# First layer: row sums of the softmax weights on GpSimd for four of eight heads, and the output projections spread over those heads

## The chip, the core and the metric

The kernel runs on one core of a Trainium2 chip. TensorE multiplies matrices, VectorE, ScalarE and GpSimd work on elements, and SyncE issues the DMAs. The metric is the device time of one execution in microseconds.

## What is computed

Two layers on x of 8 x 512 x 1024 (batch, channel, token), in float32. The first is group norm, attention with 8 heads of 64 channels, a projection and a residual; the second picks 256 tokens of each batch and runs attention over them. The change touches the first alone:

```python
h = _group_norm(x, gn_w, gn_b)
hf = h.reshape(B, C, N)
qkv = jnp.einsum('oc,bcn->bon', qkv_w, hf) + qkv_b[None, :, None]
...
attn = jnp.einsum('bhdi,bhdj->bhij', q, k) * HEAD_DIM ** (-0.5)
attn = jax.nn.softmax(attn, axis=-1)
out = jnp.einsum('bhij,bhdj->bhdi', attn, v)
...
out = jnp.einsum('oc,bcn->bon', proj_w, out) + proj_b[None, :, None]
return x + out.reshape(B, C, H, W)
```

## The kernel before

To keep float32 accuracy every operand is split into a high part that TensorE takes as it is and a low part, the rest. A product is high x high, high x low and low x high.

The first layer is one long pipeline of 512 steps: 8 batches x 8 heads x 8 steps, t = 8 h + s. In this text "head 3" is the fourth of its batch (h % 8 == 3), and T is the moment at which TensorE begins a step. A step handles 256 keys of 512 queries, so four steps are a half of a head. Per step TensorE (`step`, L477) does, in this order:

- `weigh_low(t-2)` (L473): two matmuls, p_low with the values, into the one bank `pv`;
- `scores(t)` (L446, L450): four matmuls into a ring of two; `take_max(..., 0)` (L427): one matmul of scores, the other way round, of a tile three steps ahead, for the row maxima;
- the units that the plan `PARTS` puts there: a half of a q, k, v or output ("o") projection, 12 matmuls (L371 to L373), in one step or spread over two; "vt", four transposes of v (L382); "g", group sums (L394);
- `weigh_high(t-1)` (L466, L467): four matmuls, p_high with v_high and v_low; `take_max(..., 1)` (L427).

So a step has 12 matmuls of 512 columns, and 18 or 24 with a unit. Units and row-max tiles share three banks of PSUM (2 KB in each partition). `assign_banks` gives them out by position in the matmul order, and `fill_free` makes TensorE wait until the former holder has been read.

v_high has the weights [v, 1] for each head, so that rows 0 to 63 of `pv` come out as the numerators and 64 to 127 as the denominators, every one the same sum of p (for odd heads the other way round); v_low has zeros for the ones.

ScalarE (`step`, L621): every fourth step it copies `pv` to num_den (`numer_denom`, L562); then `exps`: exp of the scores to p_high (L543) and again to p_full (L546), and the high parts of units (L575, L584, L589). VectorE (`step`, L799), one step behind: row_max of the former step's second tile (L679), every fourth step `top_of_halves` (row_max_top, L687), `p_low` = p_full - p_high (L695), row_max of this step's first tile, then the low parts of the units of the step before (q and k L708, two instructions; v L717; the residual of "o" L737), group statistics (`tile_stats`, L780), `o_low` (L792) and in step 3 `reciprocal` (L797). Each engine runs its list in order, so that what is late delays all behind it.

After a head SyncE brings the denominators into columns (`den_to_columns`), VectorE inverts them, SyncE spreads them through DRAM over the 64 rows (`rec_to_row`, `rec_to_rows`), and GpSimd multiplies (`normalise`, L878). That is nearly all that GpSimd does in this layer. Its result goes to `o_high`, `o_low` and the "o" units of the next batch, which lie in head 1 (seven whole ones) and step 0 of head 2. The reading of p_full by `p_low` is what lets ScalarE write it again two steps later.

## Time and profile before

| | us |
|---|---|
| median of 3 runs | 2790.56 (2786.41 to 2794.03) |
| the profiled execution | 2791.04 |
| its span in the profile | 2789.2 |
| TensorE (PE) busy | 2639.5, 95% |
| VectorE (DVE) busy | 2103.8, 75% |
| ScalarE (ACT) busy | 1571.9, 56% |
| GpSimd (POOL) busy | 239.1, 9% |

The first layer's steps run from 47.8 to about 2230 us of the span. Matmuls overlap in the pipeline: one is shown as some 390 ns, but the next starts about 0.23 us after it, so prices of matmuls are read from starts. Where an engine waits in the middle of an instruction (for a port, not for a semaphore), the profile shows no idle time but a longer instruction.

### The profile page before, as it was taken

The numbers are of one execution on the slowest core, as the hardware profiler recorded it, in microseconds if no ns is written. First come the engines' busy times: TensorE is split into PE (matmuls) and PEld (weight loads), VectorE is DVE, ScalarE is ACT, GpSimd is POOL, SyncE is SP. The second block draws the span as 40 slices with busy tenths as digits, with TensorE's granted clock in tenths as the row PEclk, the third lists the DMA queues.
The fourth block names the chain that finished last, engine by engine and source line by source line (L and its number), as shares of the span: only waits on it lengthen the run. The fifth ranks groups of instructions, "written<-read, shape, count | busy, mean of one in ns | idle before, by whom it ended". The sixth has DMA issues, their size and how long they took to land.

```text
span 2789.2 us, 33182 instructions
## 1 busy us (share of the span) xinstructions
PE 2639.5 (95%) x11856; PEld 2192.5 (79%) x11856; DVE 2103.8 (75%) x3294; ACT 1571.9 (56%) x1930; POOL 239.1 (9%) x134
## 2 busy tenths in 40 slices
PE   6999999999999999999999999999999985989998
PEld 5788887888888888888888888888888764777776
DVE  6888768876887688778877887688768856788753
ACT  3767646764676467656765676467656732333321
POOL 1001001100100010000000000000000121000100
PEclk9999999999999999999999999999999997999999
DMA  4522241213122412231223132312122162655443
GB/s 159 170 58 76 57 125 47 80 54 125 47 79 58 125 46 81 61 118 46 84 58 118 46 88 54 118 51 83 54 87 88 53 238 103 227 198 181 172 153 143
DMA packets 154849, 279.48 MB, mean 100 GB/s; under 512 B 51776, under 2 KB 52032, under 8 KB 154176
## 3 DMA queue, kind: packets, MB, share of 16 engines
q1 hardware_dynamic: 152128, 268.98, 30.6%
q0 software_dynamic: 2560, 8.39, 0.9%
q8 instruction: 96, 1.57, 0.2%
q14 instruction: 65, 0.53, 0.1%
HBM read 180.04 MB, written 63.18 MB: 87 GB/s over the span
## 4 chain that ended last, share of the span: by engine, by line
PE 76%; DVE 15%; issue 4%; DMA 2%; ACT 1%; SPq 1%; POOL 0%; DVEq 0%; POOLq 0%; ACTq 0%
PE tiles L371 8%; PE tiles L372 8%; PE tiles L427 8%; PE tiles L373 8%; PE tiles L473 7%; PE tiles L450 7%; PE tiles L466 7%; PE tiles L467 7%; PE tiles L446 7%; DVE p_low L695 4%; PE tiles L1304 4%; DVE row_max L679 2%; PE tiles L1354 2%; DVE flags L1546 1%; DVE flags L1544 1%
## 5 line engine op out<-in xcount | busy, mean ns | idle before, releaser
L679 DVE TENSOR_REDUCE row_max<-tiles 128x1 f32<-128x512 f32 x1014 | 695.7, 687 | 412.5 <-PE tiles L427 407.9
L543 ACT ACTIVATE p_high<-tiles 128x1024 fp32r<-128x1024 f32 x512 | 525.8, 1027 | 616.2 <-PE tiles L450 615.5
L695 DVE TENSOR_TENSOR p_low<-p_full,p_high 128x1024 fp32r<-128x1024 f32 x512 | 667.8, 1304 | 6.0 <-ACT p_full L546 5.2
L546 ACT ACTIVATE p_full<-tiles 128x1024 f32<-128x1024 f32 x512 | 521.7, 1019 | 0.0
L427 PE MATMUL tiles<-k_high_low,q_high_high 128*128 128x512 f32 x1014 | 409.7, 404 | 7.5 <-DVE row_max L679 6.9
L466 PE MATMUL tiles<-p_high,v_high 128*128 128x512 f32 x1024 | 406.8, 397 | 2.1 <-ACT num_den L562 1.3
L467 PE MATMUL tiles<-p_high,v_low 128*128 128x512 f32 x1024 | 402.2, 393 | 0.0
L427 PEld LDWEIGHTS tiles<-k_high_low,q_high_high 128*128 128x128 f32 x1014 | 313.0, 309 | 63.6 <-DVE row_max L679 22.0
L473 PE MATMUL tiles<-p_low,v_high 128*128 128x512 f32 x1024 | 326.5, 400 | 15.5 <-DVE p_low L695 15.3
L878 POOL TENSOR_TENSOR o_normed<-num_den,o_normed 64x1024 f32<-64x1024 f32 x64 | 164.4, 2569 | 2050.1 <-DMA o_normed<-rec_rows 2050.1
L450 PE MATMUL tiles<-q_low_max,k_high_one 65*128 65x512 f32 x1024 | 325.6, 399 | 0.9 <-DMA q_low_max<-row_max_top 0.8
L371 PE MATMUL tiles<-h_high,w_high 128*128 128x512 f32 x768 | 305.0, 397 | 17.6 <-DVE row_max L679 8.6
L446 PE MATMUL tiles<-q_high_high,k_high_low 128*128 128x512 f32 x1024 | 317.2, 391 | 0.0
L372 PE MATMUL tiles<-h_low,w_high 128*128 128x512 f32 x768 | 302.2, 394 | 0.0
L373 PE MATMUL tiles<-h_high,w_low 128*128 128x512 f32 x768 | 301.1, 392 | 0.0
L446 PEld LDWEIGHTS tiles<-q_high_high,k_high_low 128*128 128x128 f32 x1024 | 192.4, 188 | 47.1
L450 PEld LDWEIGHTS tiles<-q_low_max,k_high_one 65*128 65x128 f32 x1024 | 193.5, 189 | 44.1 <-DMA q_low_max<-row_max_top 2.6
L473 PEld LDWEIGHTS tiles<-p_low,v_high 128*128 128x128 f32 x1024 | 190.0, 189 | 46.7 <-DVE p_low L695 27.1
L466 PEld LDWEIGHTS tiles<-p_high,v_high 128*128 128x128 f32 x1024 | 192.8, 188 | 38.4 <-ACT num_den L562 2.2
L467 PEld LDWEIGHTS tiles<-p_high,v_low 128*128 128x128 f32 x1024 | 192.5, 188 | 37.9
L371 PEld LDWEIGHTS tiles<-h_high,w_high 128*128 128x128 f32 x768 | 146.2, 190 | 43.9 <-issue 24.2
L373 PEld LDWEIGHTS tiles<-h_high,w_low 128*128 128x128 f32 x768 | 145.5, 189 | 32.3
(167 smaller groups left out, 3169.9 us busy)
## 6 DMA issues: line engine op xcount, KB each, us to landing
x_tiles<-in_x SPq DMA_DIRECT2D x64, 512.0 KB, 4.8
w_high<-w_split SPq DMA_DIRECT2D x126, 256.0 KB, 2.8
w_low<-w_split SPq DMA_DIRECT2D x126, 256.0 KB, 2.9
k_high_one<-k_high_low SPq DMA_DIRECT2D x128, 128.0 KB, 2.3
q_high_high<-q_high_high SPq DMA_DIRECT2D x128, 128.0 KB, 2.3
o_normed<-rec_rows SPq DMA_DIRECT2D x64, 256.0 KB, 3.7
x<-x_tiles SPq DMA_DIRECT2D x32, 512.0 KB, 4.0
...
```

Of the source, the lines that this page charges most:

```text
L371: mm(fill[:, :], w1, high[:, c, cols], start=(c == 0), stop=False)
L372: mm(fill[:, :], w1, low[:, c, cols], start=False, stop=False)
L373: last = mm(fill[:, :], w2, high[:, c, cols], start=False, stop=(c == CT - 1))
L427: mm(max_bank(h, i, n)[:, :], q1[:, q_slot(h), first:first + HALF - 3:4], k1[:, k_slot(h), n * HALF:(n + 1) * HALF], start=True, stop=True ...
L446: mm(out[:, n * HALF:(n + 1) * HALF], k1[:, wk, keys[n]], q1[:, wq, queries], start=True, stop=False)
L450: last = mm(out[:, n * HALF:(n + 1) * HALF], k2[0:HD + 1, wk, keys[n]], q2[0:HD + 1, wq, queries], start=False, stop=True)
L466: mm(pv[:, :], weights_of(v1, t, n), p, start=(t % 4 == 0 and n == 0), stop=False)
L467: last = mm(pv[:, :], weights_of(v2, t, n), p, start=False, stop=False)
L473: last = mm(pv[:, :], weights_of(v1, t, n), pl[:, t % 2, n * HALF:(n + 1) * HALF], start=False, stop=(t % 4 == 3 and n == 1))
L543: nc.scalar.activation(ph[:, r, :], ring[:, r, :], ACT.Exp, scale=ATT_SCALE).then_inc(s_ph, 1)
L679: nc.vector.reduce_max(mcol[:, h % 2, n, i:i + 1], max_bank(h, i, n)[:, :], AX_X).then_inc(s_mx, 1)
L695: tt(pl[:, r, :], p32[:, r, :], ph[:, r, :].bitcast(F32), ALU.subtract).then_inc(s_pl, 1)
```

## The change

In heads 0 to 3 of each batch the denominators no longer come from ones among the weights:

- TensorE: `v_parts` holds [low, high, one] per head. With [low, high] as weights one matmul of p_high gives both products in the two halves of `pv`, so `weigh_high` has two matmuls for four. In heads 4 to 7 its two become [high, one] and, for 64 rows only, [low].
- ScalarE copies one half of `pv` to `numerators`, VectorE adds the other (`numerators`, in steps 1 and 5, before `p_low`).
- GpSimd adds the p_full tiles of a half: three adds of 128x1024 (`add_up`) and one of 128x512 (`add_tiles`), each after the `p_low` of its step. ScalarE's exp to p_full waits for the add that reads the old content.
- A unit "d" (four transposes, in step 6 and in step 2 of the next head) turns the sums, and VectorE's `denominators` sums them over 128 columns into den_columns. In heads 4 to 7 the denominators are copied alone, as one row, and come by two DMAs.
- The "o" units lie in steps 9 to 23 after the batch's start, most of them spread over two steps; k, q and v of pair 1 and a tile_stats come later; `o_high`, `o_low` of pair 0, `store` of the last tile, `reciprocal`, `rec_to_row`, `rec_to_rows` move by some steps. `normalise` waits for the `p_low` of step 4.

The planner's lists (`READ_BEHIND`, the counts in `bank_events`) and the waits of the second layer's first units are adapted to it. The diff, cut:

```diff
+SUMMED = (0, 1, 2, 3)
...
 PAIR_STEPS = (begins(0, 1, 6, 8, 2, 3, 3, 5, whole=(("k", 0), ("k", 1), ("v", 0), ("q", 1))),
-              begins(1, 3, 5, 8, 10, 12, 12, 14),
+              begins(3, 4, 9, 10, 12, 13, 14, 15, whole=(("k", 0), ("q", 0), ("v", 0))),
               begins(0, 3, 6, 8, 10, 12, 12, 14),
               begins(2, 4, 6, 8, 10, 12, 12, 14))
+OUTPUT_STEPS = {(0, 0): (9, True), (0, 1): (10, False), (1, 0): (12, False), (1, 1): (14, False), (2, 0): (16, True),
+                (2, 1): (17, False), (3, 0): (22, True), (3, 1): (23, False)}
...
+    for h in SUM_HEADS:
+        put(h, 6, ("d", h, 0))
+        put(h + 1, 2, ("d", h, 1))
...
         if kind == 0 and g > 0:
-            o = [("o", b0 - 1, t, i) for t in range(CT) for i in range(2)]
-            for s in range(7):
-                put(b, 1 + s, o[s])
-            put(a + 2, 0, o[7])
+            for (t, i), (s, whole) in OUTPUT_STEPS.items():
+                (put if whole else spread)(a + s // STEPS, s % STEPS, ("o", b0 - 1, t, i))
...
+STATS = [(3, 3), (3, 5), (3, 7), (4, 0)]
...
-READ_BEHIND = dict(m=8, k=26, q=26, v=12, vt=28, o=26, g=22)
+READ_BEHIND = dict(m=8, k=26, q=26, v=12, vt=28, o=26, g=22, d=9)
...
-                at += {"g": 1, "vt": 2}.get(u[0], 6 * len(parts))
+                at += {"g": 1, "vt": 2, "d": 2}.get(u[0], 6 * len(parts))
                 take(u)
-            at += 5
+            at += 3 if is_summed(h * STEPS + s - 1) else 5
...
+    vs = sb("v_parts", [P, 2, NT, 2, 3, HD], F32R)
...
-    nd = sb("num_den", [P, 2, N])
+    num = sb("numerators", [P, N])
+    psum = sb("p_sums", [P, N])
...
+            pe.wait_ge(s_sum, 4 * half_sum(*u[1:]) + 4)
+            for j in range(4):
+                last = nc.tensor.transpose(fill[:, j * P:(j + 1) * P], psum[:, j:HALF:4], ident[:, :])
+            last.then_inc(s_unit, 1)
...
-        def weights_of(v, t, n):
+        def weights_of(kind, t, n):
             h, j = t // STEPS, 2 * (t % 4) + n
-            return v[:, (h // 2) % 2, j, h % 2:h % 2 + 2, :].rearrange("p a d -> p (a d)")
+            blocks = dict(both=slice(0, 2), ones=slice(1, 3), low=slice(0, 1))[kind]
+            return vs[:, (h // 2) % 2, j, h % 2, blocks, :].rearrange("p a d -> p (a d)")
...
         def weigh_high(t):
             if t % 4 == 0 and t > 0:
-                pe.wait_ge(s_nd, t // 4)
+                if is_summed(t - 1):
+                    pe.wait_ge(s_num, sum_of(t - 1) + 1)
+                else:
+                    pe.wait_ge(s_den, ones_read(t - 1))
...
             for n in range(2):
                 p = ph[:, t % 2, n * HALF:(n + 1) * HALF]
-                mm(pv[:, :], weights_of(v1, t, n), p, start=(t % 4 == 0 and n == 0), stop=False)
-                last = mm(pv[:, :], weights_of(v2, t, n), p, start=False, stop=False)
+                for kind in ("both",) if is_summed(t) else ("ones", "low"):
+                    last = mm(pv[0:HD if kind == "low" else P, :], weights_of(kind, t, n), p, start=(t % 4 == 0 and n == 0 and kind != "low"),
+                              stop=False)
             last.then_inc(s_phu, 1)
...
         def weigh_low(t):
             pe.wait_ge(s_pl, t + 1)
             for n in range(2):
-                last = mm(pv[:, :], weights_of(v1, t, n), pl[:, t % 2, n * HALF:(n + 1) * HALF],
-                          start=False, stop=(t % 4 == 3 and n == 1))
+                last = mm(pv[:, :], weights_of("both" if is_summed(t) else "ones", t, n),
+                          pl[:, t % 2, n * HALF:(n + 1) * HALF], start=False, stop=(t % 4 == 3 and n == 1))
             last.then_inc(s_plu, 1)
...
+            if t > 1 and is_summed(t - 2):
+                act.wait_ge(s_sum, added(t - 2))
             nc.scalar.activation(p32[:, r, :], ring[:, r, :], ACT.Exp, scale=ATT_SCALE).then_inc(s_p32, 1)
...
-            nc.scalar.activation(nd[:, h % 2, i * HALF:(i + 1) * HALF], pv[:, :], ACT.Copy).then_inc(s_nd, 1)
+            nc.scalar.activation(num[mine, i * HALF:(i + 1) * HALF], pv[others if is_summed(t) else slice(0, HD), :],
+                                 ACT.Copy).then_inc(s_nd, 1)
+            if not is_summed(t):
+                if ones_up_to(h) > 1:
+                    act.wait_ge(s_dcol[a], 32 * (ones_up_to(h) - 1))
+                nc.scalar.activation(den[:, a, i * HALF:(i + 1) * HALF], pv[HD:HD + 1, :], ACT.Copy).then_inc(s_den, 1)
...
-            if h % 2 == 0 and h > 0 and s == 7:
+            if h % 2 == 0 and h > 0 and h % HEADS != 2 and s == 7:
                 o_high(h // 2 - 1)
+            if h % HEADS == 3 and s == 1:
+                o_high((h - 2) // 2)
...
+        def numerators(t):
+            h, i = t // STEPS, (t % STEPS) // 4
+            mine = slice(h % 2 * HD, (h % 2 + 1) * HD)
+            to = num[mine, i * HALF:(i + 1) * HALF]
+            dve.wait_ge(s_nd, t // 4 + 1)
+            tt(to, pv[mine, :], to, ALU.add).then_inc(s_num, 1)
...
+            dve.wait_ge(s_unit, unit(u))
+            if u[1] > 1:
+                dve.wait_ge(s_rec, u[1] - 1)
+            nc.vector.reduce_sum(dcol[:, a, 4 * u[2]:4 * u[2] + 4],
+                                 fill_of(u)[:, :].rearrange("p (j k) -> p j k", j=4), AX_X).then_inc(s_dsum, 1)
...
+            if h > 0 and s == 3:
+                reciprocal(h - 1)
...
+                if t % 4 == 1 and t > 1 and is_summed(t - 2):
+                    numerators(t - 2)
                 p_low(t - 1)
...
+            for u in UNITS.get((h, s), []):
+                if u[0] == "d":
+                    denominators(u)
...
-                if h % HEADS == 3 and s in (1, 3, 4, 5):
-                    tile_stats(b, (1, 3, 4, 5).index(s))
+                if (h % HEADS, s) in STATS:
+                    tile_stats(b, STATS.index((h % HEADS, s)))
...
+            if h % 2 == 1 and h > 1 and h % HEADS != 3 and s == 0:
                 o_low(h // 2 - 1)
-            if h > 0 and s == 3:
-                reciprocal(h - 1)
+            if h % HEADS == 3 and s == 2:
+                o_low((h - 2) // 2)
...
+        def add_up(t):
...
+            pool.wait_ge(s_pl, t + 1)
+            if first:
+                pool.wait_ge(s_p32, t + 1)
+                pool.wait_ge(s_on, max(h - 1 + i, 0))
+                if sum_of(t) > 0:
+                    pool.wait_ge(s_unit, unit(("d", *SUM_HALVES[sum_of(t) - 1])))
+            else:
+                pool.wait_ge(s_sum, 4 * sum_of(t) + t % 4 - 1)
+            nc.gpsimd.tensor_tensor(psum[:, :], p32[:, (t - 1) % 2, :] if first else psum[:, :], p32[:, t % 2, :],
+                                    ALU.add).then_inc(s_sum, 1)
+        def add_tiles(h, i):
+            pool.wait_ge(s_pl, h * STEPS + 4 * i + 5)
+            pool.wait_ge(s_sum, 4 * half_sum(h, i) + 3)
+            nc.gpsimd.tensor_tensor(psum[:, 0:HALF], psum[:, 0:HALF], psum[:, HALF:N], ALU.add).then_inc(s_sum, 1)
...
             pool.wait_ge(s_rb[a], 16 * (h // 2 + 1))
+            if h + 1 in SUM_HEADS:
+                pool.wait_ge(s_sum, 4 * half_sum(h + 1, 0) + 4)
...
             pool.wait_ge(s_nd, 2 * h + 2)
+            if h in SUM_HEADS:
+                pool.wait_ge(s_num, half_sum(h, 1) + 1)
...
-            nc.gpsimd.tensor_tensor(on[rows, :], nd[rows, a, :], on[rows, :], ALU.mult).then_inc(s_on, 1)
+            nc.gpsimd.tensor_tensor(on[rows, :], num[rows, :], on[rows, :], ALU.mult).then_inc(s_on, 1)
...
-        for h in range(1, ALL_HEADS):
+        for h in range(ALL_HEADS):
...
-            normalise(h - 1)
+            if h - 1 in SUM_HEADS:
+                add_up((h - 1) * STEPS + 7)
+                add_tiles(h - 1, 1)
+            if h in SUM_HEADS:
+                for s in range(1, 4):
+                    add_up(h * STEPS + s)
+                add_tiles(h, 0)
+            if h > 0:
+                pool.wait_ge(s_pl, h * STEPS + 5)
+                normalise(h - 1)
+            if h in SUM_HEADS:
+                for s in range(5, 7):
+                    add_up(h * STEPS + s)
...
+            sp.wait_ge(s_den, ones_read(h * STEPS + 7))
+            if h > 1:
+                sp.wait_ge(s_rec, h - 1)
+            for i in range(2):
+                sp.dma_start(dcol[:, a, 4 * i:4 * i + 4],
+                             den[:, a, i * HALF:(i + 1) * HALF].rearrange("o (p k) -> o p k", p=P)).then_inc(s_dcol[a], 16)
...
-                if s == 2:
+                if s == 1 and h - 1 in ONE_HEADS:
                     den_to_columns(h - 1)
+                if s == 3:
+                    rec_to_row(h - 1)
                 if s == 4:
-                    rec_to_row(h - 1)
-                if s == 5:
                     rec_to_rows(h - 1)
...
-            if h >= HEADS and h % HEADS == 2 and s == 2:
+            if h >= HEADS and h % HEADS == 3 and s == 2:
                 store(h // HEADS - 1, CT - 1)
-            if h >= HEADS and h % HEADS == 2 and s == 3:
+            if h >= HEADS and h % HEADS == 3 and s == 3:
                 after_store(h // HEADS - 1, CT - 1)
```

## Rows read from the trace of the kernel before

**Rows 1.** The page: busy time of the engines, and their shares of the last chain.
```profile
PE 2639.5 (95%) x11856; PEld 2192.5 (79%) x11856; DVE 2103.8 (75%) x3294; ACT 1571.9 (56%) x1930; POOL 239.1 (9%) x134
...
PE 76%; DVE 15%; issue 4%; DMA 2%; ACT 1%; SPq 1%; POOL 0%; DVEq 0%; POOLq 0%; ACTq 0%
```

**Rows 2.** Stretches: batch 3 by heads (0, 3, 4, sum); length, busy time by engine, clock.
```profile
861.55:898.36 36.81, 36.81 (x166) 30.90 (x165) 24.49 (x35) 23.18 (x29) 3.16 (x1) 1.00 0.18 51
...
975.58:1007.74 32.16, 31.89 (x142) 26.31 (x141) 29.80 (x50) 21.15 (x26) 3.63 (x2) 1.00 0.17 50
1007.74:1039.60 31.86, 31.62 (x137) 26.02 (x136) 25.22 (x38) 20.56 (x25) 4.26 (x2) 1.00 0.16 43
...
sum 274.53, PE 272.43 PEld 226.28 DVE 212.54 ACT 174.89 POOL 24.29; mean PE 34.05 PEld 28.28 DVE 26.57 ACT 21.86 POOL 3.04
```

**Rows 3.** The chain of waits, 942 to 952: start, length, what.
```profile
942.10 0.47 PE tiles L473 x2
...
947.61 0.47 PE tiles L473 x2
...
951.75 0.47 PE tiles L473 x2
```

**Rows 4.** Timeline of PE, 303 to 310: start, length, instruction.
```profile
303.15 0.63 PE L473 MATMUL tiles<-p_low,v_high 128*128 128x512 f32 x2
...
306.37 0.63 PE L473 MATMUL tiles<-p_low,v_high 128*128 128x512 f32 x2
...
309.15 0.63 PE L473 MATMUL tiles<-p_low,v_high 128*128 128x512 f32 x2
```

**Rows 5.** Stretches: heads 0 to 4 of batches 1 to 6, the sum.
```profile
sum 1079.95, PE 1068.37 PEld 887.69 DVE 812.57 ACT 626.08 POOL 88.31; mean PE 178.06 PEld 147.95 DVE 135.43 ACT 104.35 POOL 14.72
```

**Rows 6.** Groups of instructions on GpSimd by line: count, busy, mean.
```profile
L1780 POOL TENSOR_TENSOR wq_parts<-q_k_normed,wq_parts 128x2048 fp32r<-128x2048 f32 x1 | 4.6, 4597 | 9.5 <-ACT wq_parts L1496 9.5
```

**Rows 7.** Timelines of POOL, DVE and PE where GpSimd multiplies.
```profile
1247.64 2.40 POOL L878 TENSOR_TENSOR o_normed<-num_den,o_normed 64x1024 f32<-64x1024 f32 x1 [39.05 <-DMA o_normed<-rec_rows]
...
1247.78 2.28 DVE L687 TENSOR_TENSOR row_max_top<-row_max 128x4 fp32r<-128x4 f32 x1
...
1251.25 0.74 PE L473 MATMUL tiles<-p_low,v_high 128*128 128x512 f32 x2 [1.44 <-DVE p_low L695]
...
1254.09 0.47 PE L371 MATMUL tiles<-h_high,w_high 128*128 128x512 f32 x1 [0.92 <-DVE row_max L679]
...
299.10 2.93 DVE L695 TENSOR_TENSOR p_low<-p_full,p_high 128x1024 fp32r<-128x1024 f32 x1
...
615.21 3.36 POOL L878 TENSOR_TENSOR o_normed<-num_den,o_normed 64x1024 f32<-64x1024 f32 x1 [37.83 <-DMA o_normed<-rec_rows]
...
173.34 2.40 POOL L878 TENSOR_TENSOR o_normed<-num_den,o_normed 64x1024 f32<-64x1024 f32 x1 [26.35 <-DMA o_normed<-rec_rows]
...
173.82 1.27 DVE L780 BATCH_NORM_STATS2 bn_parts<-x_tiles 128x6 f32<-128x512 f32 x2
```

**Rows 8.** Timelines of PE, DVE and ACT in one step, T = 903.39.
```profile
903.39 0.63 PE L473 MATMUL tiles<-p_low,v_high 128*128 128x512 f32 x2
...
903.59 0.69 DVE L679 TENSOR_REDUCE row_max<-tiles 128x1 f32<-128x512 f32 x1 [0.54 <-PE tiles L427]
904.20 1.22 DVE L695 TENSOR_TENSOR p_low<-p_full,p_high 128x1024 fp32r<-128x1024 f32 x1
...
904.06 0.60 ACT L562 ACTIVATE num_den<-tiles 128x512 f32<-128x512 f32 x1 [0.23 <-PE tiles L473]
...
905.91 1.02 ACT L546 ACTIVATE p_full<-tiles 128x1024 f32<-128x1024 f32 x1
```

**Rows 9.** Timeline of DVE and POOL, 15 to 16: a handover.
```profile
15.38 0.15 DVE L753 TENSOR_SCALAR gn_small<-tiles 128x4 f32<-128x4 f32 x1
...
15.72 1.32 POOL L884 TENSOR_TENSOR gn_small<-gn_small 128x4 f32<-128x4 f32 x1 [7.51 <-DVE gn_small L753]
```

**Rows 10.** Stretch: heads 1 to 3 of batch 0.
```profile
87.64:181.31 93.67, 88.47 (x381) 73.03 (x380) 80.00 (x117) 62.70 (x76) 7.42 (x3) 1.00 0.35 110
```

More of the change, by code:

```diff
@@ L44, with is_summed, half_sum, sum_of @@
 HALF_UNITS = (0, 1)
+SUMMED = (0, 1, 2, 3)
+SUM_HEADS = [h for h in range(ALL_HEADS) if h % HEADS in SUMMED]
+ONE_HEADS = [h for h in range(ALL_HEADS) if h % HEADS not in SUMMED]
+def is_summed(t):
+    return t // STEPS % HEADS in SUMMED
+def half_sum(h, i):
+    return 2 * SUM_HEADS.index(h) + i
+SUM_HALVES = [(h, i) for h in SUM_HEADS for i in range(2)]
+def sum_of(t):
+    return half_sum(t // STEPS, t % STEPS // 4)
+def ones_up_to(h):
+    return sum(i <= h and i % 2 == h % 2 for i in ONE_HEADS)
 def begins(k0, k1, q0, q1, v0, v1, vt0, vt1, whole=()):
@@ L324, in place_use, with added, ones_read @@
         return (w, 1) if w < EARLY else (EARLY + (w - EARLY) % 2, (w - EARLY) // 2 + 1)
+    def added(t):
+        return 4 * sum_of(t) + max(t % 4, 1)
+    def ones_read(t):
+        return 2 * ONE_HEADS.index(t // STEPS) + t % STEPS // 4 + 1
     def tensor(pe, then):
```

54 lines of the change are left out of this document (35 added, 19 removed).

## The prediction

> **What bounds it now.** I read the page first: TensorE is busy for 95% of the span and holds 76% of the chain that ended last, VectorE 75% and 15% [rows 1]. Then the stretches of one batch head by head: the granted clock is 1.00 throughout and TensorE is busy for the whole of head 0 (36.81 of 36.81 us), as in heads 1 and 2; in heads 3 and 4 VectorE comes to 29.80 of 32.16 and 25.22 of 31.86 us, with TensorE still at 31.9 and 31.6 [rows 2]. Heads 0 to 2 are pure TensorE time; head 3 stands near both limits.
>
> The chain of waits gives the price of a step. It starts at the two L473 matmuls: from 942.10 to 947.61 a step with 24 matmuls takes 5.51 us, from 947.61 to 951.75 one with 18 takes 4.14; six matmuls are 1.36, one is 0.227, and a step has about 0.07 besides [rows 3]. The timeline adds that twelve matmuls and nothing else take 2.78 (306.37 to 309.15), and with four turned blocks (L382) 3.22 (303.15 to 306.37), so four transposes cost 0.45 [rows 4].
>
> **What it takes away.** Per head with a sum, a step has four value matmuls for six, in 32 heads of eight steps: 512 matmuls, 512 x 0.227 = 116 us, all on the path. It adds 64 "d" units of four transposes, 64 x 0.45 = 29 us, priced at [rows 4] since they have the shape of L382. Counting PARTS, heads 0 to 4 of a batch go from 156, 192, 144, 132, 132 matmuls to 142, 140, 146, 134, 130. With 0.227 each, 0.56 a head for its eight steps and 0.45 for each turned unit (3, 2, 2, 4, 1), and for head 4 its present 1.5 of waits, the new heads would take 34.1, 33.2, 34.6, 32.7, 32.0 = 166.6 us on TensorE alone. Now these five take 1079.95 / 6 = 180.0 in batches 1 to 6 [rows 5]. That is the ceiling, 13.4 a batch, if nothing else is late.
>
> **What GpSimd's adds cost.** A head gets six adds of 128x1024 and two of 128x512, beside the 64x1024 multiply it has. Only that multiply and two 128x2048 subtractions are in the trace: 2.40 undisturbed and 4.60 [rows 6, 7]. Both agree with a time by elements in a partition, whatever the number of partitions, so I take 2.40 and about 1.27. The Trainium skill, "GPSIMD Engine Reference", section "Elementwise — side-by-side cycle accounting", has about 2.6 cycles an element, by its 1.2 GHz an estimate of 2.2 us before dispatch; by it the waits below would shrink by some 30 us in all. The row decides.
>
> The adds run beside TensorE, but not beside all of VectorE. While GpSimd multiplied from 1247.64 for 2.40, the 128x4 row_max_top took 2.28 and ended with it; at 299.10, under another multiply, p_low took 2.93 in place of 1.22; and at 615.21, where a p_low was first, the multiply took 3.36. But two bn_stats of 512 each, begun 0.48 into the multiply at 173.34, took 1.27 together [rows 7], without a wait. So operations with two SBUF inputs (p_low, top, o_low) and GpSimd exclude each other for a whole instruction; others do not. The Trainium skill says so too ("SBUF — State Buffer", section "SBUF: two separate sides": whichever starts first has the shared pair for the whole instruction); the rows agree, with 2.28 for 4 columns.
>
> It also shows the price on TensorE: that late p_low let L473 wait 1.44, and L371, which needs the bank of a late row_max, 0.92 in the next step [rows 7].
>
> **The cycles.** In an ordinary step T is L473's start: row_max at T+0.2, p_low at T+0.8, the exp to p_full from T+2.5 to T+3.5, the unit's first matmul, after seven others, at T+1.64 [rows 8]. DVE to GpSimd takes 15.72 - 15.53 = 0.19 [rows 9]; for GpSimd to ScalarE I take 0.2 as well. An add starts when p_low is done. (a) p_low to p_low is then at least 1.22 + 0.19 + 2.40 = 3.8; a step with 16 matmuls is 3.7. (b) The first add of a half reads both p_full buffers, and the exp that refills one waits for it: 1.22 + 0.19 + 2.40 + 0.2 + 1.02 = 5.0, twice a head; behind that exp ScalarE queues the unit's evictions and the next p_high. (c) At steps 4 to 6 p_low waits for the new numerators add (ScalarE's copy ends T+1.3, then 0.68), starts at T+1.9, and before p_low of step 6 come 1.22, 0.19, 1.27, p_low 1.22, the multiply 2.40, an add 2.40, 0.2 and 1.02: 10.0 us where TensorE's two steps (3.7 + 4.15) want it after 6.8. Of the 3.2 late, 1.67 is slack (3.7 - 0.81 - 1.22): 1.6 stall a head. (d) In five places (step 2 or 6) the planner gives the unit behind "d" the bank of the row-max tile of that same step: TensorE comes at T+2.1, VectorE, which starts that row_max as p_low ends (T+2.0), has read it at T+2.7: 0.5 to 0.6 each even when on time; (c) is partly absorbed there.
>
> I walked the five heads step by step with these prices, VectorE's list with 0.61 for a row_max (903.59 to 904.20) and 1.22 for p_low [rows 8]. Stalls beyond TensorE's own time: head 0, 2.5 (step 6 1.6 by bank, 0.9 by p_low); head 1, 3.7 (1.45 where o_low waits for an add in step 0 and the row_max behind it holds the bank of step 1; 0.6, 0.6 by bank; 1.0 by p_low); head 2, 1.4 (an "o" unit of 12 matmuls in step 6 covers (c)); head 3, 4.4 (VectorE's 29.80 [rows 2] grow by four operations of 0.69, the new numerators and denominators, to 32.5, a kq_low and a residual against a tile_stats and a v_low coming out even; TensorE has 32.7); head 4, 2.7 (vt.1 and the fourth tile_stats now in its step 0). Sum 166.6 + 14.7 = 181.3, against 180.0: +1.3 a batch.
>
> **Small terms.** Heads 5 and 7: the multiply now waits for p_low of step 4, so collisions as in [rows 7] end there; between nothing and the 1.44 seen, I take 0.6 each. Heads 4 to 7 copy the denominators apart: a second ScalarE copy at about the 0.60 of L562 [rows 8]; it costs some 0.3 in head 6's step 1, which has no unit, nothing elsewhere; without a unit as cover it would be 0.3 twice a head, 1.2 a batch. Net -0.8 a batch. SyncE: den_to_columns goes a step forward and becomes two DMAs, only in heads 4 to 7; rec_to_row and rec_to_rows go a step forward, past the twins' and the row-max row's issue; the multiply they feed is held by p_low of step 4 anyway. What queues behind is load_piece, which has a unit of 12 matmuls as cover: taken at nothing, at most 1 a batch. v_parts' new stride in ScalarE's and VectorE's writes: nothing to 0.1 each, 16 a batch; nothing taken. The "low" matmul of heads 4 to 7 writes 64 rows for 128, with as many columns, so I take the same 0.227; bounds are 0.11, a transpose with a quarter of the columns [rows 4], and twice 0.227.
>
> **Sum.** Batches 1 to 6: 6 x (1.3 - 0.8) = +3. Batch 0 has no "o" units, so heads 1 to 3 fall to GpSimd's pace, 33.1 a head (p_low of step 0 to 1 2.8, then 5.0, 3.8, 3.8, 10.0 for two, 3.8, 3.8) against 93.67 for the three [rows 10]: by my walk 33.7, 33.5 and 35.5, +9; head 4 +2.5; head 0 saves 1.5: +10. Batch 7 has no tile_stats: -3.5. Total +9.5: 2791.0 (the profiled execution's own; its span 2789.2) becomes 2800.5, say 2801; the median of the runs, 2790.6, is 0.4 under the profiled one.
>
> **Rivals.** First, the adds are absorbed. If VectorE's idle time (34.05 - 26.57 = 7.5 a head [rows 2]) takes in half of the stalls, 14.7 / 2 x 8 = 59 us come back: 2742. For it: units lie in nearly every step, and a slack of 1.67 forgives (a) wholly. Against: 1.44 and 0.92 from one multiply alone [rows 7]; now there are nine GpSimd operations a head. If all are absorbed, 2791 - (13.4 + 0.8) x 8 = 2677; I give that next to nothing. Chance 0.30.
>
> Second, slower by much: at T5+4.5 p_low of step 5 comes as the 128x512 add ends (T5+4.55). If the multiply goes first, p_low of step 5 is done at T5+8.2 and the bank behind "d" at T5+8.8 for T5+5.8: 3.0 in place of 1.8 of stall in each of 4 heads, 1.2 x 4 x 8 = 38: 2839. It decides when VectorE is over 0.1 late in step 5, which head 3 is in my walk. By the same page and section of the Trainium skill the one that starts first wins; the trace has both orders [rows 7]. Chance 0.20.
>
> The forecast, gain and locks about equal (2785 to 2820): 0.50. Of it 0.2 lies within 0.3%, the least that a measurement of this kernel tells from no change, (2782 to 2799), 0.05 goes to faster and 0.25 to slower. Faster 0.35, same 0.20, slower 0.45. The range takes in the first rival's centre and the second's: 2738 to 2840.
>
> **What would show it.** TensorE has 11600 matmuls; GpSimd is busy for 239 + 32 x (6 x 2.40 + 2 x 1.27) = 780 us or more; p_low's mean is over 2 us in heads 0 to 3, its minimum still 1.2; row_max_top's mean is over 1; step 6 of heads 0, 1 and 3 is over 4.7 us, with waits of L371 for row_max and of L473 for p_low, together some 15 us a batch. Head 1 is near 37, head 3 near 37. I am wrong if p_low mostly takes 1.2 in heads 0 to 3 or heads 0 to 3 each come within 1 us of 34.1, 33.2, 34.6, 32.7 (then 2700), or if one step 6 alone is over 7 (then slower).

## The result, and the profile after

The changed kernel takes 2823.1 us (median; 2822.4 to 2824.6) and the one before 2792.3 us beside it: a ratio of 1.0113, 95% interval 1.0094 to 1.0132. It is slower by 1.1%. The forecast was 2801, slower by 0.4%, within 2738 to 2840.

The page of the changed kernel, section 1 (busy time and share by engine), and two of its costliest groups (busy time, mean of one | idle before, what ended it):

```profile
PE 2598.6 (92%) x11600; PEld 2110.1 (75%) x11600; DVE 2198.2 (78%) x3422; ACT 1613.9 (57%) x1994; POOL 785.3 (28%) x390
...
L775 DVE TENSOR_TENSOR p_low<-p_full,p_high 128x1024 fp32r<-128x1024 f32 x512 | 661.1, 1291 | 46.8 <-ACT p_full L616 45.3
L616 ACT ACTIVATE p_full<-tiles 128x1024 f32<-128x1024 f32 x512 | 523.4, 1022 | 211.4 <-POOL p_sums L989 211.3
```

TensorE has 11600 matmuls and GpSimd 785.3 us, as forecast (11600 and 780). TensorE is busy for 40.9 us less than before [rows 1] and the span is 31.6 us longer, so 72 us of new idle time stand on TensorE. What is new is ScalarE's line: its exp to p_full, which waited for nothing before, waits 211.3 us for GpSimd's adds. How much of that wait reaches TensorE the page does not say; `e_thin_mul` below does. p_low's mean has hardly moved, 1.29 us for 1.30.

Stretches, the sum for heads 0 to 4 of batches 1 to 6 (first number), which answers to [rows 5]:

```profile
sum 1090.07, PE 1031.55 PEld 837.63 DVE 889.93 ACT 635.66 POOL 501.09; mean PE 171.93 PEld 139.60 DVE 148.32 ACT 105.94 POOL 83.51
```

That is 1090.1 / 6 = 181.7 us a batch, with 180.0 before. Divided by stretches (each head from the start of its first scores matmul), the 31.6 us are: batch 0 +19.9; batches 1 to 6 +4.6 together (heads 0 to 4 +10.1, heads 5 to 7 -5.5); batch 7 +3.3; all ahead of the first step -0.5; all behind the last +4.3.

Batch 0, heads 0 and 1, after and (last two lines) before; length, busy time of PE, PEld, DVE, ACT, POOL, granted clock, DMA share, GB/s:

```profile
47.27:91.43 44.16, 37.72 (x151) 29.40 (x150) 32.79 (x41) 25.94 (x35) 13.12 (x6) 0.92 0.48 152
91.43:129.08 37.65, 26.71 (x101) 20.26 (x100) 32.77 (x41) 20.78 (x25) 19.15 (x10) 0.94 0.51 166
```
```profile
47.76:87.64 39.88, 38.04 (x161) 30.87 (x160) 27.84 (x39) 24.87 (x34) 0.00 (x0) 0.96 0.51 166
87.64:117.30 29.66, 26.16 (x109) 21.05 (x108) 25.54 (x37) 21.22 (x27) 2.63 (x1) 1.00 0.51 168
```

Two heads lose 12.3 us there, with VectorE's busy time up by 5.0 and 7.2 us. One head 1 of a later batch (batch 3), in its steps 5 to 7, shows the everyday loss. Timeline of the changed kernel: start, length, engine and line [idle before <- what ended it]:

```profile
946.96 1.22 DVE L775 TENSOR_TENSOR p_low<-p_full,p_high 128x1024 fp32r<-128x1024 f32 x1
...
947.29 3.12 POOL L1010 TENSOR_TENSOR o_normed<-numerators,o_normed 64x1024 f32<-64x1024 f32 x1 [0.22 <-issue]
...
948.92 0.47 PE L423 MATMUL tiles<-o_high,w_high 128*128 128x512 f32 x1 [0.50 <-DVE row_max L759]
...
950.63 2.40 POOL L989 TENSOR_TENSOR p_sums<-p_full 128x1024 f32<-128x1024 f32 x1 [0.23 <-POOL o_normed L1010]
...
951.99 1.06 DVE L767 TENSOR_TENSOR row_max_top<-row_max 128x4 fp32r<-128x4 f32 x1
...
953.13 1.03 ACT L616 ACTIVATE p_full<-tiles 128x1024 f32<-128x1024 f32 x1 [4.35 <-POOL p_sums L989]
954.19 1.23 DVE L775 TENSOR_TENSOR p_low<-p_full,p_high 128x1024 fp32r<-128x1024 f32 x1 [1.13 <-ACT p_full L616]
...
955.47 0.73 PE L541 MATMUL tiles<-p_low,v_parts 128*128 128x512 f32 x2 [0.54 <-DVE p_low L775]
```

The reader is to follow one chain: p_low, GpSimd's multiply behind it (3.12 us for 2.40, since it began under p_low), the first add of the half, which stands behind the multiply on GpSimd, the exp to p_full, which stood 4.35 us on ScalarE, the next p_low, and TensorE's L541.

### The profile page after: what moved, and what is told of

It is laid out like the page before. It is cut to its first block and busy times, and to the rows that moved or that the text cites. A ratio compares the mean times of both kernels' runs of the same rounds, so it can differ in the third digit from the quotient of the medians.

```text
span 2820.8 us, 33912 instructions
## 1 busy us (share of the span) xinstructions
PE 2598.6 (92%) x11600; PEld 2110.1 (75%) x11600; DVE 2198.2 (78%) x3422; ACT 1613.9 (57%) x1994; POOL 785.3 (28%) x390
## 5 line engine op out<-in xcount | busy, mean ns | idle before, releaser
L775 DVE TENSOR_TENSOR p_low<-p_full,p_high 128x1024 fp32r<-128x1024 f32 x512 | 661.1, 1291 | 46.8 <-ACT p_full L616 45.3
L616 ACT ACTIVATE p_full<-tiles 128x1024 f32<-128x1024 f32 x512 | 523.4, 1022 | 211.4 <-POOL p_sums L989 211.3
L534 PE MATMUL tiles<-p_high,v_parts 128*128 128x512 f32 (+1 forms) x1536 | 449.0, 400 | 3.8 <-ACT den_rows L640 1.5
L1010 POOL TENSOR_TENSOR o_normed<-numerators,o_normed 64x1024 f32<-64x1024 f32 x64 | 173.8, 2716 | 848.4 <-DMA o_normed<-rec_rows 426.7
L989 POOL TENSOR_TENSOR p_sums<-p_sums,p_full 128x1024 f32<-128x1024 f32 x128 | 306.9, 2398 | 260.8 <-DVE p_low L775 260.8
L541 PE MATMUL tiles<-p_low,v_parts 128*128 128x512 f32 x1024 | 329.5, 404 | 24.8 <-DVE p_low L775 24.7
L423 PE MATMUL tiles<-h_high,w_high 128*128 128x512 f32 x768 | 306.4, 399 | 23.3 <-DVE row_max L759 15.0
L534 PEld LDWEIGHTS tiles<-p_high,v_parts 128*128 128x128 f32 (+1 forms) x1536 | 255.3, 171 | 77.0 <-ACT den_rows L640 6.2
L541 PEld LDWEIGHTS tiles<-p_low,v_parts 128*128 128x128 f32 x1024 | 189.5, 189 | 62.4 <-DVE p_low L775 41.5
L989 POOL TENSOR_TENSOR p_sums<-p_full 128x1024 f32<-128x1024 f32 x64 | 153.0, 2390 | 255.5 <-DVE p_low L775 187.0
L423 PEld LDWEIGHTS tiles<-h_high,w_high 128*128 128x128 f32 x768 | 146.1, 190 | 52.0 <-issue 31.1
```

What stands on the lines that cost most here:

```text
L423: mm(fill[:, :], w1, high[:, c, cols], start=(c == 0), stop=False)
L534: last = mm(pv[0:HD if kind == "low" else P, :], weights_of(kind, t, n), p, start=(t % 4 == 0 and n == 0 and kind != "low"), stop=False)
L541: last = mm(pv[:, :], weights_of("both" if is_summed(t) else "ones", t, n), pl[:, t % 2, n * HALF:(n + 1) * HALF], start=False, stop=(t % ...
L616: nc.scalar.activation(p32[:, r, :], ring[:, r, :], ACT.Exp, scale=ATT_SCALE).then_inc(s_p32, 1)
L775: tt(pl[:, r, :], p32[:, r, :], ph[:, r, :].bitcast(F32), ALU.subtract).then_inc(s_pl, 1)
L989: nc.gpsimd.tensor_tensor(psum[:, :], p32[:, (t - 1) % 2, :] if first else psum[:, :], p32[:, t % 2, :], ALU.add).then_inc(s_sum, 1)
```

## The experiments

The code line names are those of the changed kernel. "Sum" is heads 0 to 4 of batches 1 to 6 divided by six, from stretches as above; before it is 180.0, after 181.7. The length of a step is counted between the starts of its first scores matmul and the next step's.

**First four.** `e_thin`, `e_dlast`, `e_batch0` and `e_nosum` start from the changed kernel.

```
-  tensor_tensor(psum[:, :], ..., ALU.add)           # add_up, 1024 columns
+  tensor_tensor(psum[:, 0:16], ..., ALU.add)        # 16 columns but for the very first
-  tensor_tensor(psum[:, 0:HALF], ..., ALU.add)      # add_tiles
+  tensor_tensor(psum[:, 0:16], ..., ALU.add)
```

> The changed kernel with the adds of p and the joining of the two halves of a sum done on 16 columns instead of 1024 and 512 (after the very first one), so most of the denominators of the four summed heads is left out. Every wait, unit and instruction count stays. Theory (GpSimd time of the adds, through the port that it shares with VectorE and through the exp to p_full held by the first add of a half, is what eats the gain): heads 0 to 4 of batches 1 to 6 fall from 181.5 to 167 to 172 us, batch 0 loses its 12 us in heads 0 and 1, total 2700 to 2735 (ratio to before 0.968 to 0.98). Rival (the schedule around the adds, that is the banks of the new units, the numerators on VectorE and the moved output units, eats it): it stays at 2790 or more.

Measured: 2816.0 us, ratio 1.0074 (1.0056 to 1.0092), sum 184.8. The theory fell: GpSimd's time for the adds was gone and the loss stayed. (The profiled execution is the longest of the four, 2828 us, so its sum is somewhat high.) The time lies in the rival's range, but the trace shows something else than the schedule. Timeline, step 6 of head 2 in batch 3, and the stretch behind it:

```profile
976.62 2.37 POOL L1011 TENSOR_TENSOR o_normed<-numerators,o_normed 64x1024 f32<-64x1024 f32 x1 [0.84 <-DMA o_normed<-rec_rows]
976.86 3.20 DVE L775 TENSOR_TENSOR p_low<-p_full,p_high 128x1024 fp32r<-128x1024 f32 x1
...
980.81 0.77 PE L423 MATMUL tiles<-o_high,w_high 128*128 128x512 f32 x1 [2.48 <-DVE row_max L759]
981.38 0.63 PE L424 MATMUL tiles<-o_low,w_high 128*128 128x512 f32 x1
```
```profile
981.30:986.27 4.97, 4.97 (x13) 3.83 (x12) 1.50 (x2) 0.18 (x1) 0.00 (x0) 0.50 0.01 2
```

GpSimd, early now, starts its multiply 0.24 us ahead of p_low; p_low takes 3.20 us; the row_max behind it holds the bank of the unit behind the transposes; TensorE idles 2.48 us, and then runs for 4.97 us at a granted clock of 0.50, with matmuls 0.43 us apart for 0.23. This step took 11.08 us where TensorE has 5.5 of work. In this kernel 14 such half-clock stretches stand in steps 6 of heads 0 to 2 alone; the changed kernel has 6 in the whole first layer.

```
     for u, parts: ...                    # parts_by_step
-    for h in SUM_HEADS: put(h, 6, ("d", h, 0)); put(h + 1, 2, ("d", h, 1))   # first in its step
+    (the same lines at the end: last in its step)
```

> The changed kernel with the transposes of the sums put behind the other unit of their step instead of ahead of it, so that no unit is given the bank whose row maximum is taken in the same step. Theory (each of the five places a batch costs 0.77 us of TensorE): 5 x 0.77 x 8 = 31 us less at most, 2792 to 2805. Rival (the steps with these places are also the ones in which the adds hold p_low and the exp to p_full, and the saved time is lost there): within 5 us of the changed kernel, 2818 to 2828.

Measured: 2898.1 us, 1.0367 (1.0350 to 1.0384). Neither: 75 us slower than the changed kernel; head 3 went from about 38 to 44 us. Its waits (GpSimd; us, times, longest) and the timeline of step 6 of head 3:

```profile
POOL p_sums L989 <- PE tiles L454: 104.2, 31, 4.6
```
```profile
1060.90 2.34 POOL L989 TENSOR_TENSOR p_sums<-p_full 128x1024 f32<-128x1024 f32 x1 [0.23 <-POOL o_normed L1010]
1063.33 1.02 ACT L616 ACTIVATE p_full<-tiles 128x1024 f32<-128x1024 f32 x1 [5.66 <-POOL p_sums L989]
1064.25 0.68 ACT L662 ACTIVATE v_full<-tiles,columns 128x512 f32<-128x512 f32 x1
...
1064.99 0.82 PE L490 MATMUL tiles<-k_high_low,q_high_high 128*128 128x512 f32 x1 [4.67 <-ACT v_full L662]
```

The first add of a half may not overwrite the sum before the transposes have read it; with the transposes late it waits 104.2 us in all for them (62.8 in the changed kernel). And in head 3 the row-max tile now gets the bank of the unit ahead, whose eviction (L662) stands in ScalarE's queue behind the p_full exp that waits for that add: 4.67 us of TensorE. So the place "first in the step" was needed, and a held exp is paid twice, by what is queued behind it.

```
-SUM_HEADS = [h for h in range(ALL_HEADS) if h % HEADS in SUMMED]
+SUM_HEADS = [h for h in range(HEADS, ALL_HEADS) if h % HEADS in SUMMED]
```

> The changed kernel with heads 0 to 3 of batch 0 left as they were (denominators by the ones columns), the other seven batches summed on GpSimd. Theory (batch 0 pays 20 us because VectorE still splits weights there, one piece a step, and each of these splits stretches under the adds from 0.7 to up to 2.5 us): 2823 - 20 = 2803, 2800 to 2808. Rival (the late start of batch 0 is made up for later, or comes from the changed order of its units): 2815 or more.

Measured: 2805.9 us, 1.0046 (1.0031 to 1.0060), 17 us under the changed kernel; batch 0 is at 0.0 against the kernel before (between -0.2 and +4.8 in the seven kernels that don't sum there). As expected. In batch 0 the weights are split too (L604 on ScalarE, L745 on VectorE, two SBUF inputs). Heads 0 and 1 of batch 0: VectorE's splits (shortest, median, longest in ns) and ScalarE's waits for the pieces (us, times, longest), before and after, and one split under an add:

```profile
L665 DVE TENSOR_TENSOR x_tiles<-x_tiles x11: 641/684/693, 60.0 to 105.9; 128x512 fp32r<-128x512 f32 x11
L745 DVE TENSOR_TENSOR x_tiles<-x_tiles x11: 675/1300/2516, 60.5 to 110.6; 128x512 fp32r<-128x512 f32 x11
...
ACT x_tiles L536 <- DMA x_tiles<-in_pieces: 12.2, 4, 4.5
ACT x_tiles L604 <- DMA x_tiles<-in_pieces: 12.3, 3, 4.3
...
90.01 2.52 DVE L745 TENSOR_TENSOR x_tiles<-x_tiles 128x512 fp32r<-128x512 f32 x1
```

The split takes 0.69 alone and up to 2.52 under an add. The next piece is loaded only when it is done, but ScalarE waits no longer for the pieces than before, 12.3 us for 12.2, so the loss doesn't go by the loads. It goes by VectorE: in these two heads TensorE waits 7.9 us for p_low and 6.1 for row_max, and waited 1.4 and 1.0 before. And it is the adds: with the multiply alone thinned (`e_thin_mul`, below) batch 0 takes 274.6 us, with both thinned 264.2, and 281.8 in the changed kernel.

```
-SUMMED = (0, 1, 2, 3)
+SUMMED = ()
```

> The changed kernel with no head summed: only the other order of units, weights, statistics and output units is left, and the numerators and denominators are read as before. Theory (the spread of the output units and the move of the statistics are worth a little by themselves, heads 1 and 3 get more even, heads 5 to 7 lose their collision in step 5): 2775 to 2790. Rival (this order costs time and is part of the loss): over 2795.

Measured: 2799.2 us, 1.0019 (1.0008 to 1.0030); sum 180.7. The rival's, by little: the new order is worth nothing by itself and costs 0.7 a batch in heads 0 to 4 (heads 5 to 7 gain 5.6 us in the six batches; batch 0 and batch 7 lose 3.6 each), what head 1 gains (8.0 us) being given back in heads 2, 3 and 4 (4.2, 3.8 and 2.5 in batch 3).

**Second four.** If the multiply is what GpSimd does at the wrong time, its place must matter.

```
-  tensor_tensor(on[rows, :], num[rows, :], on[rows, :], ALU.mult)           # normalise
+  tensor_tensor(on[rows, 0:16], num[rows, 0:16], on[rows, 0:16], ALU.mult)  # e_thin_mul; with e_thin's edit: e_thin_both
```

> The changed kernel with the adds of p and also GpSimd's multiply of the numerators by the reciprocals done on 16 columns (nearly all of the denominators of the summed heads and of the normalising of all heads is left out). Every wait and every instruction stays. With thin adds alone the time stayed at 2816 us, and its trace shows the multiply starting together with p_low in step 6, p_low 3.2 us long, TensorE idle behind it for 2.3 to 2.9 us, and then 7 to 13 matmuls at half clock. Theory (it is the multiply against p_low, in the one step in which TensorE's unit waits for the row maximum behind that p_low): steps 6 of heads 0 to 2 fall from 6.7, 8.0 and 11.1 us to 4.9 to 6, the half clock is gone there, 2725 to 2750 us. Rival (steps 6 are long because of the transposes and the banks, whoever holds VectorE): 2790 or more.

> The changed kernel with only the multiply done on 16 columns (the normalising of all heads is nearly all left out); the adds of p stay whole. Theory (the multiply stands ahead of the first add of the second half on GpSimd, and the exp to p_full of step 6 waits for that add): that add starts at 1.9 instead of 4.0 us into step 6, steps 6 and 7 of heads 0 to 3 lose 1 to 2 us less together, 2823 - 32 x (1 to 2) = 2760 to 2790. Rival (the adds alone fill GpSimd and hold VectorE, so the multiply only takes their slack): 2810 or more.

Measured: 2761.4 us, 0.9883 (0.9861 to 0.9905), and 2778.6 us, 0.9948 (0.9927 to 0.9969). The second is by its theory. The first lies between its theory (2725 to 2750) and its rival: steps 6 of heads 0 to 2 are 5.07, 4.91 and 6.27 us in batch 3 and the half clock there is gone, as the theory had it, but less time came back. Sums, first `e_thin_both`, then `e_thin_mul`:

```profile
sum 1054.52, PE 1021.18 PEld 837.28 DVE 845.24 ACT 638.73 POOL 58.26; mean PE 170.20 PEld 139.55 DVE 140.87 ACT 106.45 POOL 9.71
```
```profile
sum 1059.40, PE 1022.34 PEld 837.59 DVE 853.65 ACT 637.66 POOL 435.38; mean PE 170.39 PEld 139.60 DVE 142.27 ACT 106.28 POOL 72.56
```

175.8 with next to nothing on GpSimd; 176.6 with all adds and no multiply; 181.7 with both; 184.8 with the multiply alone. In batches 1 to 6 the adds alone cost 0.8 us a batch, and the multiply on top of them 5.1. The two costs don't simply add up: with the multiply there, the whole adds cost nothing more (181.7 against 184.8), since in heads 0 to 2 they hold it back until p_low has begun. In batch 0, where VectorE has its splits, the adds alone cost 10.4. ScalarE's wait for the adds is still 148.7 us with the multiply thin (10.8 with both thin), so most of the 211.3 hardly reaches TensorE.

The adds alone mostly stay in step with p_low, since an add starts when p_low ends. The multiply starts in heads 0 and 1 right behind the add of the two halves of a sum, in head 3 when its DMA lands. There it can be ahead of p_low, as in step 6 of head 3 of the changed kernel:

```profile
1020.91 2.38 POOL L1010 TENSOR_TENSOR o_normed<-numerators,o_normed 64x1024 f32<-64x1024 f32 x1 [1.09 <-DMA o_normed<-rec_rows]
1021.08 3.30 DVE L775 TENSOR_TENSOR p_low<-p_full,p_high 128x1024 fp32r<-128x1024 f32 x1
```

The multiply makes the p_low of step 7 late (in head 0 it starts at 917.41, 2.6 us into the step), and that has one more effect, in steps 0 and 1 of head 1 of the changed kernel:

```profile
918.72 2.40 POOL L989 TENSOR_TENSOR p_sums<-p_sums,p_full 128x1024 f32<-128x1024 f32 x1 [2.46 <-DVE p_low L775]
919.75 2.44 DVE L775 TENSOR_TENSOR p_low<-p_full,p_high 128x1024 fp32r<-128x1024 f32 x1
...
926.63 0.47 PE L423 MATMUL tiles<-o_high,w_high 128*128 128x512 f32 x1 [0.97 <-DVE row_max L759]
```

The add is still running when the next p_low comes; p_low takes 2.44, o_low and row_max come late behind it, and step 1 takes 6.28 us, for 5.07 in `e_thin_mul`, where that p_low takes 1.29.

```
             if h in SUM_HEADS:
+                add_up(h * STEPS + 5)
             if h > 0: ... normalise(h - 1)
-                for s in range(5, 7): add_up(h * STEPS + s)
+                add_up(h * STEPS + 6)
...                                     # and the waits between multiply and adds, to match
```

> The changed kernel with GpSimd's multiply put behind the first add of the head's second half instead of ahead of it; nothing is left out. Theory (the exp to p_full of step 6 is held by the add behind the multiply): step 6 of heads 0 to 2 comes to 4.2 to 4.5 us before the bank's 0.6, the loss in step 7 stays, 0.6 to 1.2 us a head less, 2785 to 2808. Rival (the multiply now meets p_low of step 7 and holds the second add, which holds the exp of the next head's first tile, so the loss only moves): 2818 to 2830.

Measured: 2804.0 us, 1.0048 (1.0032 to 1.0064), 19 us under the changed kernel with nothing left out. Step 6 of head 2 is 6.27 us as before, but step 7 falls from 4.10 to 3.69, head 0's from 4.50 to 3.69 and head 1's to 3.84. The theory's size was right; its guess that step 6 gains and step 7 does not was wrong. ScalarE's wait for the adds falls from 211.3 to 145.7 us.

```
 e_batch0's edit, e_mul5's edit, and in sync:
+            if h == ALL_HEADS - 2 and s == 1: early(sp)
             if h > 0: if s == 1 and h - 1 in ONE_HEADS: den_to_columns(h - 1)
-            if h == ALL_HEADS - 2 and s == 1: early(sp)
```

> Three edits at once, nothing left out: heads 0 to 3 of batch 0 not summed; the multiply behind the first add of the second half; and the second layer's early loads put on the SyncE queue ahead of the denominators of head 5 of the last batch instead of behind them. Theory (the three losses are independent): 2806 for batch 0, less what the moved multiply gives in seven batches (20 to 30 us), less 4 us where step 4 of head 6 in batch 7 falls from 8.5 to 3.8 us: 2770 to 2785, below the kernel before. Rival (the multiply's move gives nothing): 2800 to 2806.

Measured: 2786.9 us (2775.2 to 2797.9), 0.9970 (0.9954 to 0.9987), just over the range expected and under the kernel before. The third edit comes from the changed kernel's batch 7, here the SyncE queue before and after, and the changed kernel's TensorE:

```profile
2177.59 1.95 SPq L1807 DMA_DIRECT2D x_full<-x  x4
...
2188.56 0.50 SPq L943 DMA_DIRECT2D q_low_max<-row_max_top  x1
```
```profile
2205.86 1.16 SPq L1095 DMA_DIRECT2D den_columns<-den_rows  x2
2207.11 3.02 SPq L1955 DMA_DIRECT2D x_full<-x  x4
2211.26 0.52 SPq L1086 DMA_DIRECT2D q_low_max<-row_max_top  x1
```
```profile
2217.21 1.22 PE L513 MATMUL tiles<-q_low_max,k_high_one 65*128 65x512 f32 x2 [3.46 <-DMA q_low_max<-row_max_top]
...
2218.66 1.91 PE L534 MATMUL tiles<-p_high,v_parts 128*128 128x512 f32 x4
```

In the kernel before, the four loads of 512 KB were issued 11 us ahead of the row-max row. The change puts den_to_columns in front of them; the queue waits there for the denominators, the loads leave at 2207 and the small row issued at 2211.26 lands under them, some 6 us after its issue (the median of its kind is 1.9), 3.46 us late for TensorE, which then runs at half clock again: four matmuls in 1.91. Step 4 of head 6 takes 8.51 us, and 2.79 with the loads ahead (3.77 in the kernel before). It has nothing to do with GpSimd: `e_nosum` has 7.71 there and `e_thin_both` 9.69. Of the moved multiply there remained one cost, in head 3:

```profile
1008.19 2.38 POOL L1012 TENSOR_TENSOR o_normed<-numerators,o_normed 64x1024 f32<-64x1024 f32 x1 [0.22 <-issue]
1010.51 1.21 DVE L775 TENSOR_TENSOR p_low<-p_full,p_high 128x1024 fp32r<-128x1024 f32 x1
```

p_low starts as the multiply ends, step 7 takes 5.36 us, and in some batches half clock follows.

**Last four.** All start from `e_comb`.

```
+            if h % HEADS == 4 and h - 1 in SUM_HEADS: wait(s_pl, h * STEPS + 2); normalise(h - 2)
-            if h > 0:
+            if h > 0 and not (h % HEADS == 3 and h in SUM_HEADS):
                 ... normalise(h - 1)
...                                     # and the waits between multiply and adds, to match
```

> The kernel of the three edits (batch 0 not summed, multiply behind the first add of the second half, early loads ahead) and one more: the multiply that falls into head 3 is put into step 2 of head 4, where GpSimd has no adds. Nothing is left out. Theory (in head 3 the multiply starts in step 7, holds p_low there until 2.5 us and costs 1.4 to 2.5 us, at times with half clock behind it): head 3 falls from 37.6 to 35.5 to 36.2 us, head 4 stays at 33.9, 2787 - 7 x (1.4 to 2.5) = 2769 to 2777. Rival (head 3 is bound by VectorE's other work, the statistics and o_low): head 3 stays over 37, 2783 to 2790.

Measured: 2769.8 us (2767.5 to 2772.7), 0.9919 (0.9906 to 0.9933): 53 us under the changed kernel and 23 under the kernel before, by the theory. Head 3 of batch 3 in `e_comb`, then in `e_late`, and its sum:

```profile
975.79:1013.37 37.58, 34.09 (x152) 27.75 (x150) 32.81 (x47) 22.64 (x27) 19.17 (x10) 1.00 0.31 98
```
```profile
964.48:1000.71 36.23, 34.11 (x152) 27.76 (x150) 30.93 (x47) 22.16 (x27) 16.81 (x9) 1.00 0.35 107
...
sum 1066.93, PE 1024.77 PEld 837.19 DVE 883.07 ACT 637.96 POOL 488.30; mean PE 170.80 PEld 139.53 DVE 147.18 ACT 106.33 POOL 81.38
```

The sum is 177.8 a batch, and no half-clock stretch is left in the first layer's steps. Of the 17 us, 10 are head 3's (37.67 to 36.21 us in the mean of batches 1 to 6, in seven batches). The rest goes with the half clock: `e_comb`'s profiled execution has 57 matmuls of it in these steps, some in batch 0, which the edit doesn't touch. Most of what is left above the 176.6 of `e_thin_mul` is step 1 of head 1, 6.12 us for 5.07: p_low under an add, as above.

```
+                first = block and any(u[0] == "d" for u in UNITS.get((h, s), []))
+                if first: reduce_max(*block, 0)
                 p_low(t - 1)
-            if block:
+            if block and not (t > 0 and first):
                 reduce_max(*block, 0)
...                                     # e_maxf; e_all has e_late's edit too; e_three this one and
-SUMMED = (0, 1, 2, 3)
+SUMMED = (0, 1, 2)
```

> The kernel of the three edits and one more: in the steps with transposes of a sum, VectorE takes the row maximum whose bank the next unit gets ahead of p_low instead of behind it. Nothing is left out. Theory (the 0.6 us in each of the five such steps of a batch is the wait for that row maximum behind p_low, and p_low itself has room there): steps 6 of heads 0, 1 and 2 fall from 5.19, 4.92 and 6.27 to 4.3, 4.2 and 5.6 us, steps 2 of heads 1 and 3 from 4.9 to 4.3, and the time by 7 x 5 x 0.6 = 21 us, to 2762 to 2772. Rival (p_low, held 0.7 us longer, holds the add, and with it the exp to p_full and the next step): the steps stay or the next ones grow by as much, 2782 or more.

> All five edits together, nothing left out. Theory (the losses are independent): 2787 - (10 to 17) - 21 = 2749 to 2758, a ratio to the kernel before of 0.983 to 0.987. Rival (what the one frees, the other takes): 2765 or more.

> The kernel of the three edits with the row maximum ahead of p_low, and with only heads 0 to 2 of a batch summed; head 3 has its denominators by the ones columns as before. Nothing is left out. Without any sums head 3 takes 35.97 us, with them 37.6. Theory (in head 3 the sum costs more than its matmuls bring): 2767 - 7 x 1.6 = 2750 to 2760, no later than with all five edits by more than 5 us. Rival (the matmuls of head 3 are wanted): 2770 or more.

Measured: 2842.2 us, 1.0171 (1.0153 to 1.0189); 2827.1 us, 1.0125 (1.0108 to 1.0143); 2816.3 us, 1.0084 (1.0069 to 1.0098). All three by their rivals. The row maximum ahead of p_low costs 55 us. Step 6 and 7 of head 0, timeline of `e_maxf`:

```profile
904.43 0.69 DVE L759 TENSOR_REDUCE row_max<-tiles 128x1 f32<-128x512 f32 x1 [0.80 <-PE tiles L490]
905.04 1.22 DVE L775 TENSOR_TENSOR p_low<-p_full,p_high 128x1024 fp32r<-128x1024 f32 x1
905.26 0.47 PE L423 MATMUL tiles<-h_high,w_high 128*128 128x512 f32 x1 [0.40 <-DVE row_max L759]
...
912.48 0.73 PE L541 MATMUL tiles<-p_low,v_parts 128*128 128x512 f32 x2 [1.23 <-DVE p_low L775]
```

VectorE waits 0.80 us for the tile itself, which TensorE makes in this same step, and even then TensorE waits 0.40 (0.77 in `e_comb`). So p_low comes 1.5 to 1.7 us later, at 2.0 us into its step for 0.3 to 0.5, the bank gives 0.37 back in this step (0.1 in steps 6 of heads 1 and 2), and TensorE pays 1.23 for p_low in step 7 alone. Half or more of what these places cost is the distance between making a tile and reading it, not p_low in front. With this edit in all three kernels, `e_three` is 26 us under `e_maxf` and 11 under `e_all`: head 3's sum costs more than it brings there. Whether that holds without the edit was not run.

## Why the prediction was right, and where it was not

**The terms.** Heads 0 to 4 of batches 1 to 6: 181.3 forecast, 181.7 measured, +7.8 against +10.1 us together. Heads 5 to 7: -0.8 x 6 = -4.8, measured -5.5. Both stand. Batch 0: +10, measured +19.9. Batch 7: -3.5, measured +3.3. Behind the last step: 0, measured +4.3. Sum: +9.5 forecast, +31.6 in the span. The direction came out, and the walk of the steady batches, head by head too: 36.6, 36.9, 36.0, 37.1 and 34.7 forecast, 36.4, 36.8, 36.5, 38.2 and 33.8 measured, where the last two errors cancel. 17 of the 22 us that were missed are the first batch and the last. The time, 2823, is just above the band that the forecast itself gave an even chance (2785 to 2820) and inside the range, which was wide enough to take in the second rival.

**Batch 0.** The mis-sized term. The walk had GpSimd's pace for heads 1 to 3 and a saving of 1.5 in head 0; heads 0 and 1 lost 4.3 and 8.0. It left out that VectorE's list in batch 0 holds a weight split in most steps of heads 0 and 1, an operation with two SBUF inputs as the prediction's own rule asks; the eleven splits there go from 0.68 to 1.45 us in the mean, and what stands behind them is late. `e_batch0` gives 17 us back.

**Batch 7.** "SyncE: ... taken at nothing" failed. The prediction counted the queue's order against the units' loads, and not the second layer's early loads, which den_to_columns moved past. `e_comb` has that step at 2.79 us for 8.51, and batch 7 at -0.6 for +3.3.

**Behind the last step.** +4.3 here, +0.3 in `e_late`, +0.9 in `e_comb`, but +4.5 in `e_thin_both` and +2.0 in `e_mul5`. The kernels with the loads ahead mostly have the small values (one of five has +3.7), but `e_thin` has +0.7 without them. The cause stays open.

**The cycles.** (c) is right to 0.3: from the p_low that starts in step 5, at 944.47, to the one in step 7, at 954.19, there are 9.7 us for the 10.0 forecast, and TensorE's steps 6 and 7 take 9.42 for 7.85, 1.6 as forecast. But step 6 keeps its 4.91 in `e_thin_both`, so only the 0.8 of step 7 are (c); the rest is the bank, (d). (d) is right in size, 0.50 at 948.92 and up to 0.77 (in `e_comb`), and half right in cause, as `e_maxf` shows. The 1.45 forecast for head 1, where o_low and a row_max are behind an add, is 1.2, by way of a p_low of 2.44.

What the prediction made of the total was wrong. Its first rival took all of the 14.7 us of stalls a batch as what absorbed adds would give back. GpSimd's adds and multiply together cost 181.7 - 175.8 = 5.9, and with both nearly out, 175.8 - 166.6 = 9.2 us stay: 1.5 each in heads 0 to 2, 2.8 in head 3, 1.9 in head 4. They belong to the schedule and to the other new work ("d" units, numerators, denominators), which `e_thin_both` keeps; in batch 3 of `e_thin_both` TensorE waits 5.3 us for row_max in these heads and 0.2 for p_low. So the ceiling of this order of units was 4.2 us a batch, not 13.4. The first rival's far end, 2677 if all were absorbed, was out of reach without another order; 2761 was measured for it, with SyncE's loss in batch 7 still inside.

**The rivals.** The first (adds absorbed, 2742) did not happen. Nor did the second (the multiply ahead of p_low) in heads 0 to 2: there p_low goes first, as at 946.96, and the multiply takes 3.10, 3.11 and 3.17 us in the mean of each head for 2.40. In head 3 its kin does: there the multiply has started when p_low comes in step 6, that p_low takes 3.30 and the step 7.32 us. Its mechanism is what `e_thin` ran into in full.

**The signs.** p_low was to have a mean over 2 us in heads 0 to 3. In batch 3 it is:

```profile
L775 DVE TENSOR_TENSOR p_low<-p_full,p_high x32: 1206/1224/3299, 883.6 to 1028.0; 128x1024 fp32r<-128x1024 f32 x32
```

Minimum, median and longest: 1.21, 1.22 and 3.30 us. By the prediction's own words (wrong if p_low mostly takes 1.2) the lock was not where the time was expected: of the 256 p_lows of heads 0 to 3 only 24 take more than 2 us, 15 of them under the add at the turn from head 0 to 1 or 1 to 2 and 6 under the multiply in head 3. A second of its signs of being wrong came too, one step 6 over 7 us (head 3's, "then slower"), and slower it was. The waits of L371 for row_max and of L473 for p_low (now L423 and L541), forecast at some 15 us a batch together, are 4.2 and 1.2 in heads 0 to 4 of batch 3. row_max_top has a median of 0.16 and one of 1.06, for the mean over 1 forecast. Head 1 at 36.8 came as said, head 3 is 1 us over it. The rule of exclusion itself held: in the changed kernel p_low, row_max_top, o_low or a split began 72 times with 0.3 us or more of an add or multiply still to run, and always ended with it or later, such as 3.20 us in `e_thin` of p_low under a multiply that began 0.24 earlier, 1.06 of a 128x4 top here. The Trainium skill, "SBUF — State Buffer", section "SBUF: two separate sides", says the same, and the trace agrees.
